# Cross-attention and mixture-of-experts on one core: gate products formed in stage 1, projection tiles gated on GpSimd, routing in four parts

## Chip, cores and metric

One core of a Trainium2 chip. The metric is the device time of one execution in microseconds (us). Engines: TensorE (PE), VectorE (DVE), ScalarE (ACT), GpSimd (POOL); SyncE (SP) issues most DMAs.

## The reference, cut to what matters

2048 tokens of width 512. All matrix products are float32; the kernel forms most of them as three products of high and low parts.

```python
def attention(x, k, v, Wh, wg_w, wo_w, gamma, beta):       # x: layernormed, 4 heads of 128
    ...                                                    # Q, K, V by head; scores with decay, summed over the batch
    A = jnp.maximum(jnp.abs(masked.sum(axis=0)), 1.0)
    O = jnp.einsum('hst,bthe->bshe', A, V).reshape(b, s, dim)
    Y = (O - O.mean(-1)) / jnp.sqrt(O.var(-1) + GN_EPS) * gamma + beta
    W = jax.nn.relu(x @ wg_w)
    return W * Y @ wo_w

def moe(x, Wg, W1, W3, W2, Ws1, Ws3, Ws2):                 # 16 experts, 4 groups of 4
    scores = softmax(x @ Wg.T)                             # best 2 groups, then best 4 experts of them
    h = silu(x @ W1[e].T) * (x @ W3[e].T); y += combine[e] * (h @ W2[e].T)
    return y + silu(x @ Ws1.T) * (x @ Ws3.T) @ Ws2.T

x = x + attention(layernorm(x), ctx, ctx, ...)
x = x + moe(layernorm(x), ...)
```

## The kernel before

Tokens go in 16 tiles of 128. Every engine has its own instruction stream, in the order written, and semaphores tie the streams together. `pipeline(engine, 16, [(ahead, part), ...])` runs step s = ..., and in each step calls each part for tile s + ahead; the first and last steps are written out, the middle is a loop unless `ramp` is as large as the tile count. The stages follow one another:

- **Stage 1** (0 to 68 us). Each tile of x is loaded by SP (L315), normed by DVE (`norm_1`, L905), transposed by PE, split into high and low parts (ACT L541, DVE `low_1` L921) and multiplied by wg (PE L705 to L707). ACT takes the relu into `gate_out`, two buffers (L551), which waits until the store of the tile two before has landed; SP stores the tile to `gate_d` (L324). SP's step s is `load_x(s+3)`, then `store_gate(s-2)`. POOL issues the first head loads in quarters, `qdec` and the first expert set (L419 to L425), each when PE has transposed some tile. DVE's `context_sum` (L945) waits for all gate stores, since its buffer is `gate_out`.
- **Attention** (68 to 177 us), head by head. After the last head DVE takes the statistics of `o_sb` (L976, L980), ACT norms it (L587), POOL multiplies by gamma (L463) and adds beta (L465), and DVE multiplies by the gate tile `gin` (`gate_o`, L992).
- **Projection and router** (177 to 263 us). PE's step s is transposes of gated tile s+1 (`tr_a`), projection of tile s (L790 to L792, 12 matmuls), transposes of normed tile s-2 (`tr_b`) and router of tile s-3 (L810). DVE does the gating, the low part (`a_low`, L1018), the residual add (L1032), the statistics (L1034), the norm (`xr`, L1047), the low part of the first expert weights (L1025) and the copy of the logits (L1053). SP's step s is `load_gate(s+2)` (waits for `tr_a(s)`: `gin` has two buffers), `store_xn(s-2)`, `load_x3(s+1)` (waits for the residual add of tile s-1), `first_tiles`, which in step 14 issues the 16 loads of the first four tiles of the expert stage (L359).
- **Selection** (263 to 287 us on DVE): groups, maxima and indices for all 16 tiles at once (`r_groups`, `r_indices`, `r_experts`), then PE counts places (`route`), then DVE forms the slots (`r_places`, `r_slots`). Two shared tiles' work lies between.
- **Shared tiles** (263 to 395 us): PE's step is down of tile t-1, transposes of h, up of tile t+1. Beside it POOL scatters each tile to its slots, 64 indirect DMAs (L488), the last 16 of them after the second expert set is split (L482), which DVE ends in its step 11.
- **Routed tiles** (404 to about 910 us): 80 tiles; their loads wait for the whole scatter (L397). Then 16 tiles of the second shared set with the combining.

## Time and profile before

| | us |
|---|---|
| median of 3 runs | 1051.89 (1049.62 to 1054.58) |
| the profiled execution | 1050.65 |
| its span (first to last instruction) | 1049.1 |
| TensorE busy | 969.8 |
| VectorE busy | 512.1 |
| GpSimd busy | 411.9 |
| ScalarE busy | 303.5 |

Of this execution the span covers all but 1.55 us. A busy TensorE is not one at its peak: the clock that it was granted has a view of its own, and a matmul of the same shape takes about twice as long at the lower of its two levels (1.2 instead of 2.4 GHz).

### The profile page before, as it was taken

The page shows a single profiled execution, that of the slowest core. Times are in us where ns is not written, and L with a number is a line of the kernel's source. Part 1 is how long each engine was busy: PE and PEld are TensorE (multiplying, and loading weights), DVE is VectorE, ACT ScalarE, POOL GpSimd, SP SyncE. Part 2 cuts the span into 40 slices and gives each one's busy share as a digit, 9 for nine tenths or more (in the row PEclk, how much of TensorE's full clock was granted, in tenths as well). Part 3 has the DMA queues.
Part 4 walks back from the last instruction along what each step waited for, and adds up shares of the span by engine and source line. Part 5 has one row for each costly group of instructions (what it writes and reads, how often), then busy time and mean ns, then how long its engine had stood idle before and what let it go on. Part 6 is the DMA issues. An engine that isn't in the chain of part 4 may idle for free.

```text
span 1049.1 us, 18753 instructions
## 1 busy us (share of the span) xinstructions
PE 969.8 (92%) x5128; PEld 840.5 (80%) x5129; DVE 512.1 (49%) x1041; ACT 303.5 (29%) x631; POOL 411.9 (39%) x276
## 2 busy tenths in 40 slices
PE   6999998999788896999999999999999999969887
PEld 5765554788777885999999999999999999868776
DVE  5545555798755442333333333333333333427867
ACT  4441223444113221223233223233223233211211
POOL 1000004551055555435255555555555220056541
PEclk9999999899789998999999999999999999988989
DMA  6769922355466765255445553445554222367753
GB/s 211 235 234 400 384 110 106 121 171 170 157 221 220 235 247 172 89 172 168 165 140 176 180 174 111 144 165 169 172 177 162 80 80 80 102 179 221 216 175 110
DMA packets 118416, 183.59 MB, mean 175 GB/s; under 512 B 13552, under 2 KB 70896, under 8 KB 115696
## 3 DMA queue, kind: packets, MB, share of 16 engines
q1 hardware_dynamic: 104480, 103.76, 30.4%
q0 software_dynamic: 13904, 79.44, 21.9%
q8 instruction: 15, 0.25, 0.1%
q14 instruction: 17, 0.14, 0.1%
HBM read 111.85 MB, written 71.30 MB: 175 GB/s over the span
## 4 chain that ended last, share of the span: by engine, by line
PE 68%; DVE 9%; issue 7%; DMA 6%; another core or an unknown queue 4%; ACT 2%; POOL 2%; SPq 2%; DVEq 0%; ACTq 0%; POOLq 0%
PE ps L844 12%; PE ps L845 12%; PE ps L846 12%; PE ps L865 7%; PE ps L867 6%; PE ps L866 6%; PE ps L686 4%; PE ps L747 3%; PE ps L758 2%; POOL xslot_d L488 2%; DMA gin<-gate_d 2%; DVE res L1255 2%; DMA gate_d<-gate_out 1%; SPq L359 1%
## 5 line engine op out<-in xcount | busy, mean ns | idle before, releaser
L844 PE MATMUL ps<-whi,xhi 128*128 (+1 forms) x896 | 306.2, 342 | 8.8 <-DVE xlo L1090 8.4
L846 PE MATMUL ps<-whi,xlo 128*128 (+1 forms) x896 | 295.2, 329 | 0.0
L845 PE MATMUL ps<-wlo,xhi 128*128 (+1 forms) x896 | 295.0, 329 | 0.0
L844 PEld LDWEIGHTS ps<-whi,xhi 128*128 128x128 f32 x896 | 174.9, 195 | 9.5 <-issue 9.5
L845 PEld LDWEIGHTS ps<-wlo,xhi 128*128 128x128 f32 x896 | 175.4, 196 | 0.0
L846 PEld LDWEIGHTS ps<-whi,xlo 128*128 128x128 f32 x896 | 173.6, 194 | 0.0
L1074 DVE TENSOR_TENSOR hx<-ps,sg 128x352 f32<-128x352 f32 x112 | 58.7, 524 | 214.3 <-ACT sg L638 189.2
L638 ACT ACTIVATE sg<-ps 128x352 f32<-128x352 f32 x112 | 52.1, 465 | 327.8 <-PE ps L846 266.8
L1096 DVE TENSOR_TENSOR hlo<-ps,hhi 128x384 fp32r<-128x384 f32 x112 | 62.3, 556 | 172.0 <-ACT hhi L652 170.6
L865 PE MATMUL ps<-whi,hhi 128*128 (+1 forms) x333 | 134.1, 403 | 10.4 <-DVE hlo L1096 9.2
L867 PE MATMUL ps<-whi,hlo 128*128 (+1 forms) x333 | 132.5, 398 | 0.0
L866 PE MATMUL ps<-wlo,hhi 128*128 (+1 forms) x333 | 131.8, 396 | 0.0
L447 POOL CAST whi<-raw 128x2816 fp32r<-128x2816 f32 x16 | 40.5, 2534 | 207.3 <-PE ps L846 205.2
L516 POOL DMA_INDIRECT raw<-yslot_d,sloti x64 | 63.8, 997 | 119.4 <-DMA yslot_d<-ysb 71.5
L449 POOL TENSOR_TENSOR wlo<-raw,whi 128x2816 fp32r<-128x2816 f32 x16 | 100.3, 6270 | 2.4 <-POOL whi L447 0.2
L686 PE MATMUL ps<-const,hx 128*128 128x128 f32 x336 | 57.9, 282 | 34.3 <-issue 22.7
L488 POOL DMA_INDIRECT xslot_d<-scat,sloti x64 | 63.2, 987 | 66.3 <-DVE sloti L1162 26.6
L686 PEld LDWEIGHTS ps<-const,hx 128*128 128x128 f32 x336 | 43.2, 144 | 54.1 <-issue 26.9
L659 ACT ACTIVATE ysb<-ps 128x512 f32<-128x512 f32 x80 | 47.9, 599 | 131.3 <-PE ps L867 131.3
L865 PEld LDWEIGHTS ps<-whi,hhi 128*128 128x128 f32 x333 | 63.3, 190 | 25.2 <-DVE hlo L1096 10.6
L1083 DVE STREAM_TRANSPOSE ps<-xg 128x512 f32<-128x512 f32 x112 | 80.4, 718 | 6.0 <-DMA xg<-xslot_d 6.0
L652 ACT ACTIVATE hhi<-ps 128x384 fp32r<-128x384 f32 x112 | 54.5, 487 | 94.4 <-PE ps L686 46.3
(152 smaller groups left out, 1298.2 us busy)
## 6 DMA issues: line engine op xcount, KB each, us to landing
raw<-wexp_in POOLq DMA_DIRECT2D x18, 2176.0 KB, 9.7
xslot_d<-zero SPq DMA_DIRECT2D x10, 2048.0 KB, 21.0
xg<-xslot_d SPq DMA_DIRECT2D x320, 64.0 KB
yslot_d<-ysb SPq DMA_DIRECT2D x80, 256.0 KB, 2.1
xg<-xn_d SPq DMA_DIRECT2D x128, 64.0 KB
xq<-x_in SPq DMA_DIRECT2D x16, 256.0 KB, 3.5
gate_d<-gate_out SPq DMA_DIRECT2D x16, 256.0 KB, 3.0
gin<-gate_d SPq DMA_DIRECT2D x16, 256.0 KB, 2.9
```

The costliest lines, as they stand in the source:

```text
L449: pool.tensor_tensor(wlo[:, p, up], raw[:, p, up], whi[:, p, up].bitcast(F32), ALU.subtract).then_inc(w13_ready, 1)
L488: pool.indirect_dma_start(out=xslot_d, out_offset=bass.IndirectOffsetOnAxis(ap=sloti[:, t * TOPK + k:t * TOPK + k + 1], axis=0), in_=scat[ ...
L516: pool.indirect_dma_start(out=gath[:, t % GR, k, :], out_offset=None, in_=yslot_d, in_offset=bass.IndirectOffsetOnAxis(ap=sloti[:, t * TOP ...
L686: mm = pe.transpose(dst[:, k * P:(k + 1) * P], src[:, k * P:(k + 1) * P], ident)
L844: pe.matmul(ps[:, 2 + m, 0:INTER], xh, wh, start=(k == 0), stop=False)
L845: pe.matmul(ps[:, 2 + m, 0:INTER], xh, wl, start=False, stop=False)
L846: mm = pe.matmul(ps[:, 2 + m, 0:INTER], xl, wh, start=False, stop=(k == KT - 1))
L865: pe.matmul(ps[:, 5 + p, :], hh, wh, start=(k == 0), stop=False)
L866: pe.matmul(ps[:, 5 + p, :], hh, wl, start=False, stop=False)
L867: mm = pe.matmul(ps[:, 5 + p, :], hl, wh, start=False, stop=(k == IC - 1))
L1083: dve.transpose(ps[:, p, :], xg[:, r, :].rearrange("p (c k j) -> p k c j", c=NQ, k=KT)).then_inc(x_tr, 1)
L1096: dve.tensor_tensor(hlo[:, :], ps[:, 4, 0:IC * P], hhi[:, :].bitcast(F32), ALU.subtract).then_inc(h_lo, 1)
```

## The change

1. **Stage 1.** gamma and beta (`gn_sb`) are loaded right after wg. ACT's relu waits for POOL's products of the tile two before, not for its store. POOL forms relu x gamma and relu x beta for every tile (two multiplications of 128x512), and SP stores both, to `gate_d` and `gate_beta_d`. POOL's head quarters, `qdec` and the first expert set are now issued between these products.
2. **Turn of the last head.** The first tile is gated by DVE in two instructions taken between its statistics, and PE transposes it ahead of the last product of attention. The statistics of the last two groups are moved behind.
3. **Projection.** SP loads two tiles a step (`gin`, `gbin`). POOL gates tiles 1 to 15 (`gate_tile`: times o, plus gbin) and forms the low part of the first expert set; DVE loses both, and ACT takes the copy of the logits from it. SP's and DVE's streams are written out in full (`ramp=NT`), and `first_tiles` stands in SP's step 8.
4. **Selection.** It runs in four parts of four tiles; three of them lie in DVE's projection steps. PE does half an up product ahead of the last two `tr_b` and the last three routers and the other half behind them, ACT loads its Silu table there, and `route` stands in the middle of the second up product. POOL clears `hx` and waits for the stores of xn.

```diff
             for c in range(KT):
                 sp.dma_start(wg_sb[:, c, :], wg[c * P:(c + 1) * P, :]).then_inc(w1_loaded[c], 16)
+            sp.dma_start(gn_sb[:, :, :], gn[None, :, :].to_broadcast([P, 2, D])).then_inc(gn_loaded, 16)
...
             def store_gate(t, r, turn):
                 p = r % 2
-                sp.wait_ge(s1_gate, 2 + t + 1)
-                sp.dma_start(rows(gate_d, t), gate_out[:, p, :]).then_inc(gate_stored[p], 16)
+                sp.wait_ge(s1_parts, 2 * t + 2)
+                sp.dma_start(rows(gate_d, t), gate_parts[:, p, 0, :]).then_inc(gate_stored[p], 16)
+                sp.dma_start(rows(gate_beta_d, t), gate_parts[:, p, 1, :]).then_inc(gate_stored[p], 16)
...
                 sp.dma_start(gin[:, r % 2, :], rows(gate_d, r * ST + turn)).then_inc(gate_loaded[r % 2], 16)
+                sp.dma_start(gbin[:, r % 2, :], rows(gate_beta_d, r * ST + turn)).then_inc(gate_loaded[r % 2], 16)
...
-                if type(t) is int and t == NT - 2:
+                if t == 8:
                     sp.wait_ge(gated, XG)
...
-            pipeline(sp, NT, [(2, load_gate), (-2, store_xn), (1, load_x3), (0, first_tiles)], ring=B)
+            pipeline(sp, NT, [(2, load_gate), (-2, store_xn), (1, load_x3), (0, first_tiles)], ramp=NT, ring=B)
...
+            def gate_products(t):
+                p = t % 2
+                pool.wait_ge(s1_gate, 2 + t + 1)
+                pool.wait_ge(gate_stored[p], 32 * (t // 2))
+                for n in range(2):
+                    pool.tensor_tensor(gate_parts[:, p, n, :], gate_out[:, p, :], gn_sb[:, n, :], ALU.mult).then_inc(s1_parts, 1)
...
+            def gate_tile(t):
+                p = t % 2
+                pool.wait_ge(o_normed, t + 1)
+                pool.wait_ge(gate_loaded[p], 32 * (t // 2 + 1))
+                pool.tensor_tensor(gin[:, p, :], gin[:, p, :], o_sb[:, t, :], ALU.mult).then_inc(o_gamma, 1)
+                pool.wait_ge(o_gamma, t + 1)
+                pool.tensor_tensor(gin[:, p, :], gin[:, p, :], gbin[:, p, :], ALU.add).then_inc(gated, 1)
...
+            for t in range(1, NT):
+                if t == B:
+                    pool.wait_ge(wo_low, KT)
+                    pool.wait_ge(o_mm, ST * H)
+                    pool.dma_start(raw[:, 1, :], wexp[1, :, :]).then_inc(raw_loaded[1], 16)
+                gate_tile(t)
+                if t >= XR:
+                    first_low(t - XR)
...
                 if type(t) is not int or t >= 2:
-                    act.wait_ge(gate_stored[p], 16 * half)
+                    act.wait_ge(s1_parts, 2 * t - 2)
...
+            pipeline(act, NT, [(1, evac_on), (4, norm_ahead), (0, std_late), (0, std_3), (-2, evac_b_on), (0, first_high(0)), (-3, keep_logits), (0, early)])
...
+            pipeline(pe, NT, [(1, tr_a), (0, proj), (-2, tr_b_on), (-3, router_on)], ring=XR)
+            up(0, first, (0,))(0, 0, 0)
+            tr_b(NT - 2, (NT - 2) % XR, (NT - 2) // XR)
+            router(NT - 3, (NT - 3) % XR, (NT - 3) // XR)
+            tr_b(NT - 1, (NT - 1) % XR, (NT - 1) // XR)
+            router(NT - 2, (NT - 2) % XR, (NT - 2) // XR)
+            router(NT - 1, (NT - 1) % XR, (NT - 1) // XR)
+            up(0, first, (1,))(0, 0, 0)
...
+            statistics(last, 0)
+            first_centred()
+            products(last, 1)
+            rstd_o(0)
+            first_scaled()
+            statistics(last, 1)
+            products(last, 2)
+            rstd_o(1)
+            a_low(0, 0, 0)
+            products(last, 3)
+            statistics(last, 2)
...
+            pipeline(dve, NT, [(1, low_on), (0, stats_late), (0, norm_x1), (-1, norm_x2), (-3, between)], ramp=NT, ring=XR)
```

`between` calls, in steps 7 to 10, 11 to 14 and 16, `r_beaten`, `r_groups`, `r_indices` and `r_experts` of the first, second and third four tiles; the last four follow the pipeline.

## Rows read from the trace of the kernel before

**Rows 1.** Table by stage: start:end, length, busy time by engine, clock, DMA share.
```profile
16.00:44.00 28.00, 28.00 (x136) 22.49 (x135) 18.17 (x42) 14.08 (x33) 4.56 (x8) 1.00 0.82 259
207.00:256.00 49.00, 48.78 (x297) 41.80 (x297) 43.05 (x96) 21.83 (x50) 21.07 (x16) 1.00 0.53 172
```
**Rows 2.** Timeline, end of attention, PE: start, length, instruction [idle before <-releaser].
```profile
168.37 8.75 PE L758 MATMUL ps<-v_sb,at_sb 128*128 128x512 f32 x20
178.58 0.63 PE L686 MATMUL ps<-const,gin 128*128 128x128 f32 x4 [1.46 <-DVE gin L992]
182.94 1.11 PE L686 MATMUL ps<-const,gin 128*128 128x128 f32 x4 [3.74 <-DVE gin L992]
183.71 0.77 PE L790 MATMUL ps<-wo_hi,xT 128*128 128x512 f32 x1
188.55 0.58 PE L792 MATMUL ps<-wo_hi,xT_lo 128*128 128x512 f32 x1
189.32 0.48 PE L790 MATMUL ps<-wo_hi,xT 128*128 128x512 f32 x1
191.97 0.40 PE L792 MATMUL ps<-wo_hi,xT_lo 128*128 128x512 f32 x1
```
**Rows 3.** Timeline of SP, DVE and ACT in stage 1 (L319 at 16.95 loads x tile 6).
```profile
16.95 0.43 SPq L319 DMA_DIRECT2D xq<-x_in  x1
24.95 0.68 DVE L908 BATCH_NORM_STATS2 st<-xq 128x6 f32<-128x512 f32 x1
37.94 0.69 DVE L921 TENSOR_TENSOR xn_lo<-ps,xn_hi 128x512 fp32r<-128x512 f32 x1 [0.71 <-ACT xn_hi L541]
38.54 0.68 DVE L908 BATCH_NORM_STATS2 st<-xq 128x6 f32<-128x512 f32 x1
45.56 0.60 ACT L551 ACTIVATE gate_out<-ps 128x512 f32<-128x512 f32 x1 [2.32 <-DMA gate_d<-gate_out]
```
**Rows 4.** By line: landings of L319 (x), L324 (gate stores), L343 (178 to 246 us).
```profile
DMA to landing us min/median/max: 2.5/3.6/8.3
DMA to landing us min/median/max: 2.0/3.0/8.6
DMA to landing us min/median/max: 2.6/2.9/4.7
```
**Rows 5.** By line over the span: POOL's 128x512 multiplication, DVE's xn and xr (min/median/max ns).
```profile
L463 POOL TENSOR_TENSOR o_sb<-o_sb,gn_sb x16: 1252/1284/1797, 174.0 to 239.1; 128x512 f32 x16
L914 DVE TENSOR_SCALAR xq<-xq,mv,sd x16: 546/547/549, 6.4 to 59.8; 128x512 f32<-128x512 f32 x16
L1047 DVE TENSOR_SCALAR xr<-res,mv,sd x16: 546/548/1534, 194.6 to 259.0; 128x512 f32<-128x512 f32 x8, 128x512 f32 x8
```
**Rows 6.** Timeline, projection: the residual adds of tiles 3 and 15, and SP's 16 loads.
```profile
202.87 0.68 DVE L1032 TENSOR_TENSOR res<-ps,xin 128x512 f32<-128x512 f32 x1
256.05 0.69 DVE L1032 TENSOR_TENSOR res<-ps,xin 128x512 f32<-128x512 f32 x1 [1.28 <-PE ps L792]
251.01 8.87 SPq L359 DMA_DIRECT2D xg<-xn_d  x16
```
**Rows 7.** Timeline, selection: PE's router of tile 12, DVE, PE's third up product, POOL.
```profile
256.29 0.96 PE L810 MATMUL ps<-wr_sb,xT 128*128 128x16 f32 x8
263.66 0.42 DVE L1115 TENSOR_REDUCE gsc<-logits 128x64 f32<-128x256 f32 x1
275.26 0.87 PE L686 MATMUL ps<-const,hx 128*128 128x128 f32 x3 [6.04 <-issue]
285.68 0.41 PE L844 MATMUL ps<-whi,xhi 128*128 128x352 f32 x1
287.32 1.47 POOL L488 DMA_INDIRECT xslot_d<-scat,sloti  x1 [26.55 <-DVE sloti L1162]
```
**Rows 8.** Timeline, shared tiles: POOL's last wait for the split, PE's first routed matmul.
```profile
371.11 0.58 POOL L483 DMA_DIRECT2D raw<-wexp_in  x1 [4.22 <-DVE wlo L1025]
403.72 0.66 PE L844 MATMUL ps<-whi,xhi 128*128 x1 [8.36 <-DVE xlo L1090]
```

More of the change, by code:

```diff
@@ L759, in products, with tr_a, first_tr_a @@
                     mm.then_inc(o_mm, 1)
+            def tr_a(t, r, turn):
+                p = r % 2
+                if type(t) is int and t == 0:
+                    return
+                pe.wait_ge(gated, t + 1)
+                if type(t) is not int or t >= 2:
+                    pe.wait_ge(a_lo, t - 1)
+                transposes(ps[:, p, :], gin[:, p, :], KT, a_tr)
+            def first_tr_a():
+                pe.wait_ge(gated_first, 1)
+                pe.wait_ge(v_ready, ST * H)
+                pe.wait_ge(sum_ready, H)
+                transposes(ps[:, 0, :], gin[:, 0, :], KT, a_tr)
             queries(0)
@@ L773, in _ @@
             pe.wait_ge(sum_ready, H)
-            def tr_a(t, r, turn):
-                p = r % 2
-                pe.wait_ge(gated, t + 1)
-                if type(t) is not int or t >= 2:
-                    pe.wait_ge(a_lo, t - 1)
-                transposes(ps[:, p, :], gin[:, p, :], KT, a_tr)
             def proj(t, r, turn):
@@ L838, in fn @@
                     pe.wait_ge(w13_ready, need)
-                    for m in range(2):
+                    for m in halves:
+                        if base == 0 and type(t) is int and t == 0:
+                            pe.wait_ge(x1_ready, NT - 1 + m)
                         for k in range(KT):
@@ L893, in routed, with last, up_on @@
                 return bass.ds((need + 1) % 2, 1), need
-            first, last = (lambda t, place: (0, 1)), (lambda t, place: (1, NW))
-            pipeline(pe, NT, [(0, route), (-1, down(0, first)), (0, tr_h(0)), (1, up(0, first))], ring=XG)
+            def last(t, place):
+                return 1, NW
+            def up_on(t, r, turn):
+                if type(t) is int and t == 1:
+                    up(0, first, (0,))(t, r, turn)
+                    route()
+                    up(0, first, (1,))(t, r, turn)
+                elif type(t) is not int or t:
+                    up(0, first)(t, r, turn)
+            pipeline(pe, NT, [(-1, down(0, first)), (0, tr_h(0)), (1, up_on)], ring=XG)
             pe.wait_ge(rt_done, 1)
@@ L1021, in first_low @@
[L1021 to L1026 removed]
+                statistics(h, 3)
+            last = H - 1
+            products(last, 0)
+            statistics(last, 0)
+            first_centred()
@@ new lines, in _, with low_on, stats_late @@
+            products(last, 1)
[7 more added lines that the diff above has]
+            statistics(last, 2)
+            def low_on(t, r, turn):
+                if type(t) is not int or t:
+                    a_low(t, r, turn)
+            def stats_late(t, r, turn):
+                if type(t) is int and t == 0:
+                    statistics(last, 3)
+                    rstd_o(2)
+                    rstd_o(3)
```

392 lines of the change are left out of this document (242 added, 150 removed).

## The prediction

> **What bounds the kernel now.** First the busy times (table above): TensorE is busy 92% of the span, so the change can only win where TensorE waits or runs at its lower clock. The table by stage says where it has nothing to give: in stage 1 it is busy 28.00 of 28.00 us, with the DMA engines at 0.82, and in the projection from 207 us on 48.78 of 49 [rows 1]. Then the timeline of TensorE for its gaps. Behind attention it waits 1.46 and 3.74 us, and its first projection (183.71 to 188.55+0.58, 5.42 us) runs at the lower level; the next takes 3.05 us (189.32 to 191.97+0.40) [rows 2]. So a drop of the clock costs 5.42 - 3.05 = 2.4 us. At the selection there is a gap of 6.04 us, at the end of the shared tiles one of 8.36 [rows 7, 8]. The change is aimed at the two turns, before and behind the projection; it pays in stage 1 and in the projection, the two stages in which TensorE had no slack.
>
> **Stage 1.** Removed: ACT's wait for the store of the tile two before, which held it 2.32 us once [rows 3]. Added per tile: two multiplications on POOL, 2 x 1.28 = 2.57 us [rows 5], a store of 256 KB more and, for the first eight tiles, a head quarter issued between them. The period of a tile is (38.54 - 24.95)/4 = 3.40 us [rows 3], so POOL has room. It reads SBUF while DVE norms. With POOL idle L914 never took more than 0.549 us; L1047, the same form with one source in SBUF, took up to 1.534 beside POOL's work [rows 5]. A collision so costs DVE up to 0.99 us. DVE waits 0.71 us per tile for ACT [rows 3], so the ends are 0 and 14 x (0.99 - 0.71) = 4 us; a collision at its worst in every tile is unlikely, and I take 0.
>
> The Trainium skill (SBUF — State Buffer, Who interferes with whom) says that a VectorE instruction in a two-port mode and a GpSimd instruction exclude each other for their whole length, the second one waiting. The row agrees in kind. By that rule, if every norm waited for a whole product, DVE would need its 2.69 us and 1.28 more, 3.97 per tile, and 14 tiles would lose 8 us.
>
> The second cost is a queue. SP issues `load_x(t+6)` behind `store_gate(t)`, and the store now waits for POOL's products instead of the relu: 2.57 us later, and one more issue (about 0.5 us, 8.87/16 [rows 6]). Tile 6 of x was issued at 16.95 and first used at 24.95 us [rows 3], 8.0 us; 4.9 are left for its landing, and DVE's 0.71 before TensorE feels it: 5.6. The median landing is 3.6 us, the longest 8.3 [rows 4]. A landing of 8.3 then costs 2.7 us and a clock drop, 5 us; but the old kernel stopped in the same transfers too (the 2.32 us wait, with a drop perhaps 4). Ends: -4 (the old stop goes) and +10 (rival B). I take +2, since the bytes per tile rise where the DMA share is 0.82 already.
>
> The tail of stage 1: the last stores are issued some 3 us later, and `context_sum` waits for them. But POOL now issues the first expert set only behind the last product, where before it lay beside that store; if the stores land in the median 3.0 us instead of near the longest, 8.6 [rows 4], `context_sum` starts about where it did. I take 0; the other end is 5.6.
>
> **The turn of the last head.** TensorE does its 20 pieces of L758 in 8.75 us, 0.43 each [rows 2], and has done 12 of them at 168.37 + 5.1 = 173.5. The first gated tile is ready near 174.5 (sum, statistics, one product, next sum, reciprocal, second product, at the old durations, an estimate). So TensorE waits 1 us, transposes (0.6) and does the last 8 pieces (3.4): 178.6. Projection 0 starts at 179.1 instead of 183.71, at full clock, and ends at 181.9 instead of 189.1. What is late next: the statistics moved behind. Two groups' statistics (1.5 us each), two reciprocals and the residual add of tile 0 now stand ahead of ACT's `std_3(0)`, and ACT evacuates tile 2 only behind that. So projection 1 ends near 185.2 and projection 2 starts near 187.9: a gap of 2.2 us, which can drop the clock (2.4). Projection 3 then starts 4 to 6 us earlier than before, and the short gaps of the old kernel at tile 4 give 0.9 more. If the expert set (2.2 MB) that POOL now issues at tile 4 holds up the gate loads, it is 3. I take -6.
>
> **The projection.** Its old pace is (256.05 - 202.87)/12 = 4.43 us a tile [rows 6], set by TensorE [rows 1]. The new loop for `gin`: transposes of tile t (0.6), two issues (0.8), landing 2.9 [rows 4], POOL 2 x 1.28 [rows 5], then the transposes of tile t+2: 6.9 us, against two tiles' 8.9. With the longest landing, 4.7 [rows 4], it is 8.7: hidden, with 0.2 to 2 us to spare. POOL's 2.57 and the low part of 272 columns (0.7, from 512 columns) fit in 4.43. DVE loses two instructions and gets a selection part of about 1.1 us: no cost.
>
> What is moved past this loop is `first_tiles`. Its 16 issues hold SP for 8.87 us in the old trace, where no gate load was queued behind them [rows 6]. In step 8 the load of gated tile 11 is. It is wanted 0.8 us after SP turns to the batch and goes out 8.87 us after (7.4 if an issue takes 0.46): 6.6 to 8.1 us late, of which the loop's slack hides about 2. The transposes of tile 11 wait 4 to 6 us, and the clock drops (2.4). 6 to 8.5 us; I take +7.
>
> **The selection.** Old: from 263.66 to the first scatter at 287.32, and TensorE starts its third up product at 285.68, which is 28.4 us behind the end of the router of tile 12 (256.29+0.96) [rows 7]. New, from that same point: half an up product to 1.9; transposes and routers, with ACT's evacuations and table load between, to 5.8; the other half to 7.7. DVE: third part from 2 to 8, last part to 12.8, with a quarter of the elements in each instruction (the whole takes 0.42 us in L1115 [rows 7]; a part some 3.8 us, an estimate at 0.2 us for each small instruction). h is multiplied at 10.9, so TensorE still has a gap, about 3.2 us instead of 6.04, and then half an up product at the lower clock. Route ends at 16, the first slots at 20.5, the third up product starts at 21.2: TensorE is 7.2 us ahead and the scatter 9. Do the 9 count? No: POOL's last sixteen scatters wait for DVE's step 11 (4.22 us idle at 371.11 [rows 8]), and everything up to the first routed matmul hangs on that step, so TensorE's shift decides, and the gap of 8.36 us stays. Ends -4 and -10; I take -7.5.
>
> **Sum.** +2 - 6 + 7 - 7.5 = -4.5 us. Against the profiled execution, 1050.65 us (span 1049.1 and 1.55 around it), that is 1046.2; this execution lies 1.24 us under the median, 1051.89, and against that I forecast 1047.4 us, 0.4% faster. About 0.5%, 5.3 us, is what a measurement of this kernel can tell from no change.
>
> **Rivals.**
> A. The batch in step 8 is hidden (0.25). If TensorE reaches tile 11 later than by my count, or the issues go faster, +7 becomes 0: 1040.4. Against it: 16 issues are longer than a whole tile, and there are two buffers.
> B. Stage 1 becomes bound by its transfers (0.18). Place: the x loads of tiles 8 to 15 and the last stores. It decides once an x load takes over 5.6 us; 8.3 has been seen [rows 4]. Price: two stops of 2.7 us and two clock drops, 10 instead of 2, and the last store at 8.6 instead of 3.0, 5.6 more: +13.6, so 1061.0, slower than before.
> C. The projection runs at its `gin` loop (0.12). The two transfers land in 5.5 us instead of 2.9: the loop is 9.5 us, 0.3 a tile, 3.6 over 12 tiles, and small gaps pull the clock down once or twice, 2.4 to 4.8: 1047.4 + 7 = 1054.4.
> D. The selection gives nothing (0.05): the fourth part comes too late and h with it, so that the gap of 6.04 us stays where it was: 1047.4 + 7.5 = 1054.9.
>
> **How the numbers follow.** My own sum has a chance of 0.40 and a range of 1042 to 1053. The range that is to hold the time reaches from A with the better end of stage 1 (1040.4 - 4 = 1036) to B (1061). Faster by over 0.5% (below 1046.6): nearly all of A and 0.4 of my own case, 0.24 + 0.16 = 0.40. Slower by over 0.5% (above 1057.2): most of B and a little of C and D, 0.14 + 0.04 = 0.18. Within 0.5%: 0.42.
>
> **What would show it.** Stage 1: L914's mean over 0.55 us, the DMA share near 1, a gap of TensorE where x is late. Turn: the first L790 at 179 us at full clock, and a gap ahead of the third projection. Projection: a gap of 4 to 6 us ahead of the transposes of tile 11, SP's 16 loads in front of its gate load, then matmuls at twice their length. Selection: the first scatter 20.6 us behind the router of tile 12, and the gap of 8.36 us as before. I am wrong if there is no gap at tile 11 (A), if stage 1 ends over 8 us late (B), or if TensorE stops elsewhere among the shared tiles than before.

## The result, and the profile after

| | before | changed |
|---|---|---|
| median, us | 1053.24 (1049.62 to 1055.88, 4 runs) | 1065.17 (1063.49 to 1065.99, 4 runs) |
| profiled execution: time, span | 1050.65, 1049.1 | 1065.05, 1063.5 |

The ratio is 1.0114, interval 1.0079 to 1.0149: slower by 1.1%, and 4 us above the upper end of the range. In the profile the work is the same and the waits are not. The page's busy times of the changed kernel:

```profile
PE 970.3 (91%) x5128; PEld 838.2 (79%) x5129; DVE 502.8 (47%) x1030; ACT 304.7 (29%) x647; POOL 461.7 (43%) x323
```

TensorE is as busy as before (969.8 us), GpSimd 50 us more. The table by stage, its columns as in [rows 1]:

```profile
16.00:44.00 28.00, 26.53 (x127) 20.67 (x126) 17.47 (x39) 13.78 (x32) 22.62 (x22) 1.00 0.76 240
207.00:256.00 49.00, 37.81 (x207) 32.41 (x208) 26.41 (x68) 19.02 (x47) 29.19 (x27) 0.86 0.63 204
```

The two stages in which TensorE had no slack [rows 1] now have it: 1.5 of 28 us, 11 of 49, and a granted clock of 0.86. The timeline of the changed kernel up to the fourth projection (columns as in [rows 2]; TensorE, then the queue, VectorE or GpSimd behind each wait):

```profile
71.81 0.38 PE L809 MATMUL ps<-head_in 128*128 128x128 f32 x1 [0.69 <-ACT gate_out L599]
74.72 0.43 SPq L337 DMA_DIRECT2D gate_beta_d<-gate_parts  x1
85.05 2.29 DVE L1077 TENSOR_REDUCE ctx_sum<-head_in 128x4 f32<-128x2048 f32 x1 [7.62 <-DMA gate_beta_d<-gate_parts]
88.39 1.19 PE L828 MATMUL ps<-gate_out,const 128*128 128x512 f32 x1 [7.98 <-DVE gate_out L1080]
...
186.00 0.66 PE L775 MATMUL ps<-const,gin 128*128 128x128 f32 x4 [0.61 <-DVE gin L1123]
190.28 0.48 PE L889 MATMUL ps<-wo_hi,xT 128*128 128x512 f32 x1
200.28 0.50 PE L889 MATMUL ps<-wo_hi,xT 128*128 128x512 f32 x1 [2.96 <-DVE xT_lo L1128]
196.55 0.58 POOL L507 DMA_DIRECT2D raw<-wexp_in  x1
197.26 0.33 SPq L361 DMA_DIRECT2D xin<-x_in  x1
197.63 0.43 SPq L355 DMA_DIRECT2D gin<-gate_d  x1
198.10 1.24 SPq L356 DMA_DIRECT2D gbin<-gate_beta_d  x1
208.00 1.26 POOL L488 TENSOR_TENSOR gin<-gin,o_sb 128x512 f32<-128x512 f32 x1 [10.87 <-DMA gbin<-gate_beta_d]
210.72 1.12 PE L775 MATMUL ps<-const,gin 128*128 128x128 f32 x4 [5.37 <-POOL gin L490]
```

Attention's start in the trace of the kernel before:

```profile
68.75 0.49 PE L720 MATMUL ps<-head_in 128*128 128x128 f32 x2 [0.69 <-ACT gate_out L551]
78.69 1.10 PE L739 MATMUL ps<-gate_out,const 128*128 128x512 f32 x2 [1.37 <-DVE gate_out L954]
```

Four delays stand here. Stage 1 ends 3.1 us later: the first matmul behind it is at 71.81, in the old trace at 68.75. The last store of the beta product, issued at 74.72, holds `context_sum` until 85.05, so it took 10.3 us, and L828, at 78.69 in the old trace (there L739), is at 88.39: 9.7 later, 6.6 of them here. The third projection waits 2.96 us. And tile 4's gate loads go out only at 197.63, behind the load of x at 197.26, and GpSimd, which needs both of them, starts on the tile at 208.00; TensorE waits 5.37 us for it.

Later in the same timeline:

```profile
238.23 7.51 SPq L372 DMA_DIRECT2D xg<-xn_d  x16
245.78 0.43 SPq L355 DMA_DIRECT2D gin<-gate_d  x1
252.46 1.12 PE L775 MATMUL ps<-const,gin 128*128 128x128 f32 x4 [6.63 <-POOL gin L490]
280.88 0.96 PE L909 MATMUL ps<-wr_sb,xT 128*128 128x16 f32 x8
294.81 0.52 PE L775 MATMUL ps<-const,hx 128*128 128x128 f32 x3 [1.38 <-issue]
303.10 0.43 PE L929 MATMUL ps<-whi,xhi 128*128 128x352 f32 x1 [0.33 <-DVE xlo L1227]
303.33 1.04 POOL L536 DMA_INDIRECT xslot_d<-scat,sloti  x1 [15.45 <-DVE sloti L1308]
411.65 0.97 POOL L536 DMA_INDIRECT xslot_d<-scat,sloti  x1 [0.30 <-issue]
423.40 0.56 PE L929 MATMUL ps<-whi,xhi 128*128 x1 [2.94 <-DVE xlo L1227]
```

Set against rows 6 to 8, how late the changed kernel is at each point:

| point | before | changed | late |
|---|---|---|---|
| residual add of tile 3 | 202.87 | 216.30 | +13.4 |
| residual add of tile 15 | 256.05 | 281.50 | +25.5 |
| router of tile 12 ends | 257.25 | 281.84 | +24.6 |
| third up product | 285.68 | 303.10 | +17.4 |
| first store of the scatter | 287.32 | 303.33 | +16.0 |
| last store of the scatter | 394.03 | 411.65 | +17.6 |
| first routed matmul | 403.72 | 423.40 | +19.7 |
| end of the span | 1049.1 | 1063.5 | +14.4 |

The selection is the only part that gives something back before the routed tiles, 7.2 us. The 5.3 us behind the first routed matmul are the part of this comparison that no edit of the change touches; they lie behind the routed tiles, among the combining tiles, where both kernels show stops of ScalarE like those that experiments 7, 8 and 11 are about.

### The profile page after: what moved, and what is told of

The parts are those of the page before. It is cut to its first block, busy times and chain, and to the rows that moved or that the text cites. A ratio compares the mean times of both kernels' runs of the same rounds, so it can differ in the third digit from the quotient of the medians.

```text
span 1063.5 us, 18643 instructions
## 1 busy us (share of the span) xinstructions
PE 970.3 (91%) x5128; PEld 838.2 (79%) x5129; DVE 502.8 (47%) x1030; ACT 304.7 (29%) x647; POOL 461.7 (43%) x323
## 3 DMA queue, kind: packets, MB, share of 16 engines
q0 software_dynamic: 13904, 79.44, 21.9%
## 4 chain that ended last, share of the span: by engine, by line
PE 71%; DVE 8%; issue 6%; DMA 5%; another core or an unknown queue 4%; POOL 3%; ACT 2%; SPq 1%; POOLq 0%; DVEq 0%; ACTq 0%
PE ps L931 12%; PE ps L929 12%; PE ps L930 12%; PE ps L981 6%; PE ps L983 6%; PE ps L982 6%; PE ps L775 4%; PE ps L836 3%; PE ps L849 3%; DMA gate_beta_d<-gate_parts 2%; DVE res L1441 2%; DMA gbin<-gate_beta_d 2%; POOL gate_parts L437 1%; PE ps L813 1%
```

## The experiments

Runs 1 to 4 took the three delays that the change's own order of issue seemed to make, one at a time and together. Each ratio is to executions of the kernel before on the same chip, and its interval is 4 to 16 us wide. A trace is of one execution, so its stretches can differ by a few us between traces of kernels that do the same there: from the residual add of tile 0 to that of tile 5, e4, e7 and e8, which issue the same until then, take 24.3, 25.7 and 22.8 us.

**e1: the first expert set behind the last stores.**

```diff
             pool.wait_ge(s1_tr, XR + NT)
+            for side in range(2):
+                pool.wait_ge(gate_stored[side], 32 * (NT // 2))
             pool.dma_start(raw[:, 0, :], wexp[0, :, :])...
```

> The changed kernel, but GpSimd issues the load of the first expert set only when all gate stores have landed. In the changed kernel that load (2.2 MB) is issued at 74.27 us, beside the last two stores; the beta store lands 10.3 us after its issue and the context sum starts at 85.05. Theory T1 (the set's bytes are what the last store waits for): it lands in about 3 to 4 us, the context sum starts at 78 to 79, TensorE's gap of 7.97 us shrinks to about 1.4, and the kernel is 5.5 to 6.5 us faster than the changed one (about 1059). Rival R1 (the store is slow by its own doubled bytes, by wo and by the zero fill that SP queues behind it): it lands after 8 to 10 us as before, and the time stays within 1.5 us of 1065.

Measured: 1058.49 us, ratio 1.0107 (1.0029 to 1.0185). The timeline of e1:

```profile
76.97 2.29 DVE L1079 TENSOR_REDUCE ctx_sum<-head_in 128x4 f32<-128x2048 f32 x1 [0.78 <-DMA gate_beta_d<-gate_parts]
80.31 1.10 PE L830 MATMUL ps<-gate_out,const 128*128 128x512 f32 x2 [1.14 <-DVE gate_out L1082]
```

TensorE's wait of 7.98 us is 1.14, as expected, and the sum starts 8.1 us earlier than at 85.05, 1.2 of which were there at the end of stage 1 already (70.57). From there to L830 it takes 9.7 us, before 9.9 and in the changed kernel 16.6: the 2.2 MB set, issued 0.45 us ahead of the last store, was what made it land late. How much of this arrives in the time is not shown: the ratio of the changed kernel was measured twice, 1.0114 and 1.015 (e12), so by the ratios e1 is 0.7 to 4.5 us better, within their intervals, and by the plain medians, of different chips, 6.7.

**e2: the second expert set ahead of the gated tiles.** GpSimd issues it before its first gated tile instead of at tile 4.

```diff
+            pool.wait_ge(wo_low, KT)
+            pool.dma_start(raw[:, 1, :], wexp[1, :, :]).then_inc(raw_loaded[1], 16)
             pool.wait_ge(gated_first, 1)
...
-                if t == B: (the same load)
```

> The changed kernel, but the load of the second expert set is issued ahead of the first gated tile, as in the old kernel, and not at tile 4. In the changed kernel TensorE waits 5.36 us at the transposes of tile 4, whose gate loads were issued at 197.63 and 198.10, just behind the set's (196.55), and landed near 208. Theory T2 (the set's bytes delay them): they land 3 us after their issue, the gap is 0 to 1 us and the clock drop behind it (2 us) goes: 6 to 8 us faster than the changed kernel. Rival R2 (they are issued too late: SP stood at load_x3 of tile 2, which waits for tile 0's residual add, until 197.26): a gap of 1 to 2 us and the clock drop stay, 3 to 4 us faster.

Measured: 1058.78 us, ratio 1.0102 (1.0058 to 1.0146). The timeline of e2:

```profile
212.33 0.66 PE L773 MATMUL ps<-const,gin 128*128 128x128 f32 x4 [3.40 <-POOL gin L490]
```

The two gaps of 2.96 and 5.37 us are now one of 1.57 (196.42) and one of 3.40. From the residual add of tile 0 to that of tile 5 it takes 221.90 - 196.59 = 25.3 us instead of 225.35 - 196.55 = 28.8, the 3 to 4 us that the rival gave it. But nothing of them is left at the end of the projection: the residual add of tile 15 is at 281.24, in the changed kernel at 281.50 and in its second trace (e12) at 281.23. By itself this edit shows no gain, in the trace or in the ratio.

**e3: the first tiles' 16 loads spread, four in each of SP's steps 8 to 11.**

```diff
-                if t == 8:
+                if 8 <= t < 8 + XG:
+                    r = t - 8
                     sp.wait_ge(gated, XG)
-                    for r in range(XG):
-                        sp.wait_ge(xn_stored[r], 16)
-                        load_tile(0, xn_d)(r, r, 0)
+                    sp.wait_ge(xn_stored[r], 16)
+                    load_tile(0, xn_d)(r, r, 0)
```

> The changed kernel, but the 16 loads of the first four expert-stage tiles go out four at a time in SP's steps 8 to 11 and not all in step 8. Theory T3 (the batch holds back the gate load of tile 11): the gap of 6.64 us ahead of its transposes shrinks to 0 to 1 us and the matmuls behind it keep their length: 7 to 9 us faster than the changed kernel. Rival R3 (the gin loop has no slack left, so that four loads a step delay every tile): four gaps of 1 to 2 us in steps 10 to 13, 0 to 3 us faster.

Measured: 1056.6 us, ratio 1.0082 (1.0046 to 1.0118). The timeline of e3:

```profile
288.17 0.52 PE L775 MATMUL ps<-const,hx 128*128 128x128 f32 x3 [1.37 <-issue]
```

The gap of 6.63 becomes two, of 1.37 (at 247.38) and 1.49 (at 253.56), and the first transposes of h come at 288.17 instead of 294.81, or 293.02 in the second trace of the changed kernel (e12): 5 to 7 us earlier, so the batch cost about what the prediction gave it, 7.

**e4: the three together.**

> The changed kernel with the three edits of the runs beside it together. If each removes its own loss and the losses add: 6 + 7 + 8 = 21 us faster than the changed kernel, about 1044, faster than the old one by some 9 us. If one loss only hides behind another (the scatter or the shared tiles catch up), less: 1050 or more.

Measured: 1051.29 us, ratio 1.0024 (0.9988 to 1.006). The timeline of e4:

```profile
275.04 0.52 PE L775 MATMUL ps<-const,hx 128*128 128x128 f32 x3 [1.38 <-issue]
330.43 0.46 ACT L688 ACTIVATE sg<-ps 128x352 f32<-128x352 f32 x1 [12.66 <-remote]
379.16 0.46 ACT L688 ACTIVATE sg<-ps 128x352 f32<-128x352 f32 x1 [14.61 <-remote]
```

At 275.04 it stands 19.8 us ahead of the changed kernel and where the old kernel stood [rows 7]. The time fell by only 14 (by the ratio it is 9 to 13 us), and it did not come out below the kernel before, against the 1044 that was expected. Of the 19.8 us 16.1 are left at the first routed matmul (407.33) and 11.3 at the end of this trace, whose execution lies 2.5 us over the median. The first loss is in the shared tiles, where ScalarE stopped for 12.66 and 14.61 us with its inputs long ready (the last up product before the first stop had ended at 319.6); the second is behind the first routed matmul, where nothing differs between the two kernels.
**e5: the load of x behind the gate loads, on top of e4.**

```diff
-  [(2, load_gate), (-2, store_xn), (1, load_x3), (0, first_tiles)]
+  [(2, load_gate), (0, load_x3), (-2, store_xn), (0, first_tiles)]
```

> The three edits together (e4) and one more: in SP's steps of the projection the load of x for the residual add of tile s is issued in step s behind the gate loads of tile s+2, instead of ahead by one tile, so that no gate load is queued behind a wait for a residual add. Theory (the gate loads of tile 4 are late because SP stands in the wait for tile 0's residual add, which the moved statistics delay): the two gaps of TensorE ahead of tiles 2 to 4 that are left, 1.07 and 2.37 us with a clock drop, shrink to under 1 us together, the small waits of 0.6 to 0.9 for POOL's products in the loop go as well, and the first transposes of h come 3 to 6 us earlier than e4's 275.04. Rival (the bytes of the gate loads and of the expert set beside them set it, whatever the order): the gaps stay within 0.5 us of those, and the residual add is 1 us later for nothing. By either the shared tiles may give it back, since their stops of 12 us in ScalarE are not explained yet.

Measured: 1045.04 us, ratio 0.9969 (0.9928 to 1.0011), whose interval overlaps e4's. The first transposes of h are at 271.84, 3.2 us earlier, as expected. But the two larger gaps, 1.56 and 2.37 us in e4, did not shrink; only the third, of 1.08 ahead of a projection, is gone:

```profile
184.96 0.66 PE L775 MATMUL ps<-const,gin 128*128 128x128 f32 x4 [1.50 <-POOL gin L492]
199.90 1.12 PE L775 MATMUL ps<-const,gin 128*128 128x128 f32 x4 [2.73 <-POOL gin L492]
```

From the residual add of tile 0 to that of tile 5 it takes 24.2 us (209.36 - 185.12), in e4 24.3 (211.31 - 187.03): with the set already moved, the order of SP shows no gain there, and this part of the theory falls for e4. Of the 3.2 us, 1.9 were there at the residual add of tile 0 (185.12 against 187.03), ahead of anything the edit touches, and 1.3 come behind tile 5.

**e6: the second store of stage 1 left out, on top of e4.**

> The three edits together (e4), and the second store of stage 1 left out (beta's products are formed but not kept; the projection reads the gamma product in both places, so beta's term is wrong in the output). GpSimd's work in stage 1 and everything behind it stay. Theory (stage 1 costs 3 us more because the added 4 MB meet DMA engines that are busy 0.82 of the time, so that the loads of x land later): the last gate matmul of stage 1 ends at 68 to 69 us instead of 71.1, the load of x lands in 3.5 us instead of 4.0, and the stops of TensorE at 35 and 54 to 57 us go. Rival (GpSimd's products delay VectorE at SBUF, or the store waits for the products and the next load of x stands behind it on SP's queue): stage 1 still ends at 70 to 71.

Measured: 1045.3 us, one execution. The timeline of e6, the first matmul behind stage 1:

```profile
66.76 0.49 PE L808 MATMUL ps<-head_in 128*128 128x128 f32 x2 [0.69 <-ACT gate_out L598]
```

It is 5.0 us ahead of the changed kernel's (71.81) and 2.0 ahead of the old one's, with GpSimd's two products still there. VectorE's idle time for loads of x, 4.7 us in the changed kernel's stage, is 0.8. All traces together say the same: the first matmul behind stage 1 is at 70.3 to 73.5 us in the eleven with two stores a tile, and at 66.5 to 68.8 in the six with one. So the second store costs stage 1 some 5 us, 4.2 to 5.3 against the three traces of this chip with both (e5, e7, e8), and the products next to nothing: e6, with them, is 0.3 us from e13, e11 and e14, without. Whether the store costs by its 4 MB or by its place on SP's queue ahead of the load of x, this run does not part; it takes both away.

**e7 and e8: the scatter left out, and the scatter with plain stores, on top of e4.**

```diff
-                    pool.indirect_dma_start(out=xslot_d, out_offset=..., in_=scat[:, t % XR, :], ...)
+                    pool.dma_start(xslot_d[o:o + P, :], scat[:, t % XR, :])        (e8; none in e7)
```

> The three edits together (e4), and the 64 indirect stores that scatter the tokens to their slots are left out (the routed tiles then read zeros; their number and their instructions are the same). The question is what holds ScalarE for 5 to 15 us at a time among the shared tiles with all that it waits for long done, in every kernel so far. Theory R (the stops come from GpSimd's indirect stores or the transfers that they start): they are gone, and from the first transposes of h to the first routed matmul it takes 110 to 116 us instead of 132.3, the sum of the stops less. Rival I (they belong to ScalarE's own stream, its instructions or function changes): they stay, with 20 to 27 us of idle time in all, and the stage takes 125 us or more. The first routed tile needs only the second expert set then, so the end of the stage says nothing of the scatter itself.

> The three edits together (e4), and each of the 64 indirect stores replaced by a plain store of the same tile from the same GpSimd queue to a fixed place (the tokens are then not sorted by expert, so the routed part of the output is wrong). The bytes are the same; what is gone is the indirection. Theory R1 (the stops of ScalarE come from the transfers, 16 MB beside the loads of the shared tiles): they stay, 20 us or more in all. Theory R2 (they come from the indirect form): they go as without the scatter, and the stage takes 110 to 118 us.

Measured: 1026.89 us and 1023.91 us, one execution each, beside 1049.94 for the kernel before. The table by stage, from the first transposes of h to the first routed matmul, of e4, e7 and e8:

```profile
275.00:407.00 132.00, 102.92 (x569) 92.90 (x569) 64.23 (x133) 31.29 (x67) 64.87 (x66) 0.91 0.64 213
```
```profile
280.00:384.00 104.00, 100.00 (x569) 91.66 (x567) 63.77 (x129) 31.18 (x67) 1.33 (x2) 0.98 0.37 104
```
```profile
275.00:378.00 103.00, 99.33 (x568) 91.07 (x566) 63.25 (x126) 30.86 (x67) 35.09 (x66) 0.99 0.80 267
```

No ScalarE stop without a releaser is left in this stage of either, and it takes 104 to 105 us instead of 132, less than the 110 that was expected at best. e8 moves the same bytes, more per us than e4 (DMA share 0.80 against 0.64). So the stops come with the indirect form of GpSimd's stores and not with the bytes moved. That form is two things here, the indices that GpSimd works through (64.87 us busy instead of 35.09) and rows that go to scattered places, and no run parts them. Among the combining tiles, where GpSimd still issues 64 indirect loads in both runs, the stops stay: six of 43.6 us in all in e7, six of 42.4 in e8, the first of e7 being this one:

```profile
910.67 0.46 ACT L685 ACTIVATE sg<-ps 128x352 f32<-128x352 f32 x1 [10.81 <-remote]
```

**e9: part 1 undone, on top of e5.** Stage 1 stores the relu alone. GpSimd does three operations a tile (times gamma, plus beta, times the gate tile), VectorE the low part of the first expert set. The GpSimd lines below are in short form.

```diff
-                sp.dma_start(rows(gate_d, t), gate_parts[:, p, 0, :])...
-                sp.dma_start(rows(gate_beta_d, t), gate_parts[:, p, 1, :])...
+                sp.dma_start(rows(gate_d, t), gate_out[:, p, :])...
...
+            def affine(t): o_sb[t] *= gamma; o_sb[t] += beta          (GpSimd, a tile ahead)
             def gate_tile(t):
-                gin *= o_sb[t]; gin += gbin
+                gin *= o_sb[t]
```

> The order of e5 (the three edits and the load of x behind the gate loads), and part 1 of the change undone: stage 1 stores the relu alone, as the old kernel did, and GpSimd multiplies by gamma, adds beta and multiplies by the gate tile in the projection, three operations a tile of which only the last needs the load; VectorE takes the low part of the first expert set back. Theory (the doubled store is what costs stage 1 its 3 to 5 us, since without the second store e6 ended the stage at 66.1 instead of 71.1): the stage ends at 66 to 68.5, one gate load a tile instead of two shortens the loop of the gate tiles, the gaps ahead of tiles 2 and 4 that e5 still has (1.5 and 2.7 us) fall under 1 us each, and the kernel takes 1037 to 1042 us, 3 to 8 less than e5 and about 1% under the kernel before. Rival (the products were worth their bytes, since GpSimd now has 3 x 1.3 = 3.9 us in a tile of 4.43 and VectorE 0.5 more): TensorE waits 0.5 us or more for GpSimd or VectorE in most tiles, its clock falls in the projection, and the time is e5's 1045 or more.

Measured: 1002.45 us (12 runs) against 1001.01 (17 runs) for the kernel before on this chip, ratio 1.0007 (0.9986 to 1.0027). The timeline of e9:

```profile
248.54 0.51 PE L874 MATMUL ps<-wo_hi,xT 128*128 128x512 f32 x1 [3.74 <-DVE xT_lo L1113]
386.88 0.66 PE L914 MATMUL ps<-whi,xhi 128*128 x1 [9.58 <-DVE xlo L1220]
```

Stage 1 ended at 68.39, as expected, but the time is the rival's: TensorE waits for VectorE, which does pieces of the expert set and parts of the selection in one step, though in four tiles and not in most (four gaps, 8.3 us). And this chip is another one in kind: the kernel before takes 1001 us instead of 1050, and no kernel shows a ScalarE stop without a releaser on it.

**e10: the changed kernel with SP's new order alone (same chip as e9).**

> The changed kernel with one edit: SP issues the load of x for the residual add of tile s in step s, behind the gate loads of tile s+2. Theory (SP stands in the wait for tile 0's residual add): the gate loads of tile 4 go out at a_tr of tile 3, some 3 us earlier than 197.6, and TensorE's gap of 5.36 us ahead of tile 4's transposes falls to 2 to 3 us though the second expert set still lies beside them; with e2 (3.41, that set moved and the order kept) the two causes then have about half each. Rival (the 2.2 MB of the expert set are the cause): the gap stays at 5 us or more. The batch in step 8 stays, so the gap of 6.6 us at tile 11 does too.

Measured: 1015.09 us, one execution, beside 1001.01 for the kernel before. The timeline of e10:

```profile
203.28 0.60 PE L775 MATMUL ps<-const,gin 128*128 128x128 f32 x4
209.50 0.90 PE L775 MATMUL ps<-const,gin 128*128 128x128 f32 x3 [1.04 <-POOL gin L490]
```

Tile 4's transposes (203.28) have no wait at all, though the expert set still lies beside the loads; 1.04 us are lost at tile 5. From tile 0's residual add to tile 5's: 219.04 - 194.67 = 24.4 us, against 28.8. So neither the coupling through SP's queue nor the set was enough to make the whole gap: taking away either of the two (24.4 here, 25.3 in e2) gives back 3.5 to 4.4 us, and taking away both (24.2 in e5) hardly more. The batch in step 8 still costs a gap of 5.79 us, as expected. This execution, 14 us above the kernel before on a chip without ScalarE's stops, also suggests that the change costs its time there too.

**e11: the kernel before without its scatter (same chip as e9).**

> The kernel before with its 64 indirect stores left out (routed tiles read zeros, in the same number). Theory (the stops of ScalarE among the shared tiles belong to these stores in both kernels and have nothing to do with the change): no stop of 3 us or more is left in ScalarE between 275 and 395 us, the stretch from the first transposes of h to the first routed matmul takes 103 to 108 us instead of 128.5, and the kernel some 20 to 25 us less than with them. The gap of 8.36 us ahead of the first routed tile goes or becomes 2.9, since no load waits for a scatter. Rival (the stops are in the old kernel for another reason): stops of 5 us and more are left.

Measured: 993.09 us, one execution, 8 below the median of the kernel before, not 20 to 25. The stretch from the first transposes of h to the first routed matmul is 104.6 us, as expected, but the experiment could not decide what it was made for, since this chip has no such stops to take away. What it shows is the price of the scatter where it has none: TensorE waits 2.94 us at the first routed tile, and e9, with the scatter, 9.58.

**e12 and e13: the changed kernel and the kernel before once more, on one chip.**

> The changed kernel as it is, once more. Where ScalarE's long stops among the shared tiles are present, the theory gives the first result again, 1.0 to 1.3% slower than before, with TensorE late at the first routed tile. Where they are absent (kernel before near 1001 us), the scatter of 64 stores, about 92 us from its first store to the first routed tile, is what ends last: the gap of TensorE ahead of the first routed tile is then 9 to 12 us instead of 2.9, and the change costs what the scatter starts later, 303.1 - 287.3 = 15.8 us, so 12 to 16 us (1.2 to 1.6%) as well. Rival (on such a chip TensorE's gaps are swallowed by the gap at the end): the change costs under 5 us there.

> The kernel before as it is, for its trace beside the others on the same chip. Where ScalarE's stops are absent: its shared tiles take 104 us from the first transposes of h (as with the scatter left out) and not 128.5, TensorE then waits 8 to 12 us for the first routed tile, and the combining tiles behind the routed ones take some 24 us less. Where they are present: it is the trace of before again, 128 us and stops of 20 us or more in all.

Measured: e12 1065.05 us, ratio 1.015 (1.009 to 1.0211), the median of the kernel before 1048.3; this chip has the stops. e13 is one execution of 1045.12 us. The timelines of e12 and of e13, at the same four points:

```profile
72.43 0.49 PE L809 MATMUL ps<-head_in 128*128 128x128 f32 x2 [0.69 <-ACT gate_out L599]
88.98 2.05 PE L828 MATMUL ps<-gate_out,const 128*128 128x512 f32 x2 [7.95 <-DVE gate_out L1080]
293.02 0.52 PE L775 MATMUL ps<-const,hx 128*128 128x128 f32 x3 [2.81 <-issue]
418.84 0.65 PE L929 MATMUL ps<-whi,xhi 128*128 x1 [8.74 <-DVE xlo L1227]
```
```profile
66.50 0.49 PE L720 MATMUL ps<-head_in 128*128 128x128 f32 x2 [0.69 <-ACT gate_out L551]
76.73 1.10 PE L739 MATMUL ps<-gate_out,const 128*128 128x512 f32 x2 [1.66 <-DVE gate_out L954]
274.70 0.87 PE L686 MATMUL ps<-const,hx 128*128 128x128 f32 x3 [5.90 <-issue]
396.93 0.66 PE L844 MATMUL ps<-whi,xhi 128*128 x1 [7.95 <-DVE xlo L1090]
```

The same places again: +5.9 at the end of stage 1, +12.3 at the context sum, +18.3 at the selection, +21.9 at the first routed matmul. e13 had no stop in stage 1, so the doubled store costs 5.9 here. At the first routed matmul TensorE waits 8.74 us in e12, not the 2.94 that was expected. What the changed kernel itself costs on a chip without the stops was not measured, since e12 landed on another; e10 is the nearest to it.

**e14: e9 with the low part divided; e15: e5 again, on that chip.** In e14 VectorE takes the first four pieces of the low part, before the selection's parts begin, and GpSimd the other twelve, from tile 8 on.

> e9 (the relu alone stored, three operations a tile on GpSimd) with the low part of the first expert set divided: VectorE takes its first four pieces, before the selection's parts begin, and GpSimd the other twelve, from tile 8 on. Theory (e9 lost its gain to VectorE, which stood behind pieces and selection parts: gaps of 2.11, 1.37, 1.08 and 3.74 us for the low part of the gated tiles): these gaps go, the first transposes of h come at 268 to 271 us instead of 275.7, and it takes 4 to 7 us less than e9 relative to the kernel before, so a ratio of 0.993 to 0.997. Rival (GpSimd at 3 x 1.3 + 0.8 = 4.7 us a tile is now over the 4.43 of TensorE): gaps of 0.3 us and more for GpSimd in tiles 8 to 15, two clock drops, and the ratio stays at 1.0.

> e5 once more (four edits of order in the changed kernel, both products stored), beside e14 on the same chip. By the theory that the second store costs 3 to 5 us it takes 1 to 5 us more than e14; by the rival (the products are worth their bytes) it takes less than e14. Its ratio to the kernel before was 0.997 on a chip with ScalarE's stops; without them the scatter starts about as early as before's, and it should be 0.995 to 1.0.

Measured: e14 1039.5 us (12 runs), ratio 0.9912 (0.9877 to 0.9947); e15 1043.36 us (10 runs), 0.997 (0.9931 to 1.001). The timelines of e14 and of e15:

```profile
66.51 0.49 PE L808 MATMUL ps<-head_in 128*128 128x128 f32 x2 [0.69 <-ACT gate_out L599]
221.62 0.79 PE L888 MATMUL ps<-wo_hi,xT 128*128 128x512 f32 x1 [2.59 <-DVE xT_lo L1127]
270.70 0.52 PE L774 MATMUL ps<-const,hx 128*128 128x128 f32 x3 [1.38 <-issue]
```
```profile
70.27 0.49 PE L809 MATMUL ps<-head_in 128*128 128x128 f32 x2 [0.69 <-ACT gate_out L599]
270.11 0.87 PE L775 MATMUL ps<-const,hx 128*128 128x128 f32 x3 [2.81 <-issue]
```

e14 is faster than both kernels, by 0.9% than the one before and by a little more than the 0.3 to 0.7% that was expected. It is 3.8 us ahead behind stage 1 and has lost them by the selection, to two waits for VectorE of 2.6 and 2.7 us. Between e14 and e15 the traces show no difference at 270 us that would explain 4 us of median (expected were 1 to 5), and their intervals overlap: which of the two is the better is open.

## Why the prediction was wrong

The terms as forecast, and as the two traces give them (the "late" column of the table above, by its differences):

| stretch | forecast | measured |
|---|---|---|
| stage 1 | +2 | +3.1 |
| its tail, to the context sum | 0 | +6.6 |
| turn of the last head, to tile 3 | -6 | +3.7 |
| projection, tile 3 to tile 15 | +7 | +12.0 |
| to the router of tile 12 | 0 | -0.9 |
| selection | -7.5 | -7.2 |
| shared tiles | 0 | +2.3 |
| routed and combining tiles | 0 | -5.3 |
| sum | -4.5 | +14.4 |

The three steps that failed are the tail, which was put at nothing, the turn, which was to gain and lost, and the projection, which was too small.

**Stage 1, +2.** It was +3.1, and against a kernel before that has no stop in this stage +5.9 (e12, e13). The term was mis-sized: I set the gain of the old stop, up to 4, against the second store and came out near zero. The store alone cost 5.0 (e6), and the old stop was worth 2.3 (68.75 against 66.50 in e13). Of VectorE and GpSimd colliding I took 0, and that held: the norm takes 0.596 us in the mean instead of 0.547, 14 x 0.05 = 0.7 us in all, and VectorE has the slack. By the rule of the Trainium skill (SBUF — State Buffer, Who interferes with whom) it could have been 8. The trace agrees with the rule in kind and not with that price: the six norms that took 0.58 to 0.74 us are those that began while 0.3 to 0.45 us of a product were left, and none met a whole product. e6, with the products kept, ends stage 1 2 us ahead of the old kernel, so here the products did not cost it.

**Tail of stage 1, 0.** The step that failed is "if the stores land in the median 3.0 us": +6.6 (+6.3 in e12). I saw that POOL would issue the expert set only behind the last product, and concluded that the last store would land in the median time because the set no longer lay beside it. The order is the other way round: POOL has its product done first, so the set goes out 0.45 us ahead of the store that waits for that same product, and the store lands behind it in 10.3 us, longer than any in [rows 4]. The end that I had named, 5.6, was the better value. e1 shows it by moving the set behind the store. A step that makes a large transfer wait for the same event as a small one puts the two side by side, however late that event is.

**Turn of the last head, -6.** This is the largest miss, 9.7 us. The first half was nearly as forecast: tile 0's transposes wait 0.61 us, and the first projection starts 190.28 - 9.7 = 180.6 on the old clock instead of 183.71, at full clock; forecast 179.1. The third projection's wait is 2.96, forecast 2.2, and it still starts 2.3 us earlier than before (200.28 - 9.7 = 190.6, before 192.85). The step that failed is "projection 3 then starts 4 to 6 us earlier than before": the fourth starts 4.1 us later (211.49 - 9.7 = 201.8, before 197.63). I had followed the late statistics to TensorE and not to SP: they delay tile 0's residual add, SP's load of x waits for that add, and tile 4's gate loads are queued behind the load of x. I had priced the expert set beside them at 3 if it mattered. Most of the gap needed queue and set together: with either one taken away the stretch from tile 0 to tile 5 is 3.5 to 4.4 us shorter (e2, e10). But the gain at tile 5 was not kept by e2, as said there.

**The projection, +7.** From tile 3 to tile 15 it was +12.0. The batch in step 8 is in it as forecast: 16 issues in 7.51 us, a gap of 6.63 (forecast 4 to 6), then a clock drop; e3 gets 5 to 7 back. Around it the residual adds of tiles 9 and 10 stand 13.06 us apart, 8.6 over the pace. The other 3.4 us have the size of rival C (3.6) and come beside my case, not instead of it: small waits for GpSimd's second operation, of which 1.1 us is idle time (33.60 - 32.77 and 28.80 - 28.50 in the two stretches beside the batch), and a granted clock that is lower in both:

```profile
211.40:245.00 33.60, 32.77 (x189) 28.03 (x188) 20.86 (x50) 15.46 (x38) 19.83 (x18) 0.94 0.58 187
253.20:282.00 28.80, 28.50 (x164) 24.41 (x163) 22.87 (x60) 10.40 (x28) 15.78 (x15) 0.95 0.45 139
```

That is the table by stage of the changed kernel again; before, the clock was 1.00 there [rows 1]. C's own condition, two loads that land in 5.5 us, was not met: the second one of a tile lands in 3.8 us at the median and 5.3 at most. What sets these waits no run shows. They do not go with the batch: from tile 5 to tile 15 the old kernel takes 44.2 us, the changed one 56.2, and the six traces with the batch spread and both stores kept (e3, e4, e5, e7, e8, e15) 48.3 to 55.4.

**The selection, -7.5.** From the router of tile 12 to the third up product 21.3 us (forecast 21.2) instead of 28.4, TensorE's gap 1.38 instead of 6.04 [rows 7], the first store of the scatter 21.5 behind the router (forecast 20.6). This part held.

**Who releases the first routed tile.** I argued that TensorE's shift decides. The rows say otherwise: the last store of the scatter and the first routed matmul are 9.7 us apart in the old trace (394.03, 403.72), and again in e12 (409.19, 418.84), e13 (387.25, 396.93) and e10 (389.92, 399.55), with TensorE waiting 8 to 11 us in each. Only where TensorE comes later than that is the distance longer (11.75 in the changed kernel, 18.6 in e4, both with stops of ScalarE ahead of it) and the gap the 2.94 that is left without a scatter. So the start of the scatter counts as much as TensorE's shift. In the sum it made no difference, since the two are within 1.5 us of each other.

**The rivals.** B had the right places, and its chance of 0.18 was too low. Its two terms were 10 and 5.6; measured are 3.1 and 6.6. In stage 1 of the changed kernel an x load took up to 6.9 us to land, over B's 5.6, and TensorE waited 2.18 us once, with one drop of the clock behind it (matmuls of 0.63 us instead of 0.39 from 58.51 to 61.49), where B had two waits of 2.7 and two drops; in the tail the cause was the expert set and not the bytes of the stage. What brought the time above B's 1061 is that both came together with the queue at tile 4, the batch and the small waits. They were priced as cases of which one happens; they add. The lower end of the range, which played no part, was also added up wrongly: my sum held +2 for stage 1, so A with -4 in its place is 1034.4, not 1036.

## What to carry to other kernels

When a wait is moved, follow it into every queue that has an instruction behind it, SP's loads included, and look at what else the same event releases: a 2.2 MB load issued half a microsecond ahead of a 256 KB store cost 7 us in a place that was counted at nothing. Here a stage in which the bottleneck engine had no gap and the transfers were busy at 0.82 paid 3 to 6 us for another 4 MB that was to save work later, and the kernel without them (e14) was the only one clearly faster than before. Mechanisms that don't exclude one another belong into the sum or the range together, not one to a rival.

## What the runs showed of the hardware that was not expected

- ScalarE stopped for 3 to 15 us at a time, some 70 us per execution in both kernels (before: 44.1 + 29.0 us in 11 stops), with all inputs ready, and only in the two stages in which GpSimd issues indirect transfers. With 64 plain stores of the same bytes in place of the scatter, or none, the stops among the shared tiles were gone and the stretch was 28 us shorter (132 to 104), while the stops beside the indirect loads of the combining tiles stayed. On one of the chips there were none, and the kernel before took 1001 us instead of 1047 to 1053. What in the indirect form holds ScalarE, and why not on every chip, is open.
- The landing of a 256 KB store went from 2.3 to 10.2 us within one stage, the longest with the 2.2 MB load beside it.
- GpSimd's multiplications beside VectorE's norm cost it 0.05 us in the mean and 0.19 at most (0.735 instead of 0.547), not a wait of their whole length.
